# Attention over graph edges: the comparison that builds the incidence matrix reads its row of numbers from PSUM in place of SBUF

## The reference

```python
h = (x @ W).reshape(N, HEADS, HEAD_DIM)
e = leaky_relu(a_src[src] + a_dst[dst])          # one score for each edge and head
e = exp(e - segment_max(e, dst)[dst])
alpha = e / segment_sum(e, dst)[dst]
out = segment_sum(alpha[:, :, None] * h[src], dst)   # over the edges of each target node
```

## Time and profile before

| | us |
|---|---|
| median of 3 runs | 4344.1 (4341.25 to 4345.91) |
| the profiled execution, in all | 4370.65 |
| its span in the trace | 4368.8 |
| busy: PE 3282.1, DVE 2921.5, POOL 2098.1, ACT 1557.5 | |

### The profile page before, as it was taken

How to read it: one execution, slowest core, us unless ns; L and a number is a source line. 1 busy time by engine, 2 the same in 40 slices (tenths; PEclk the granted TensorE clock), 3 DMA queues, 4 the chain that set the end, 5 groups by cost and what they waited for, 6 DMA issues and landing times. The chain is left out here.

```text
span 4368.8 us, 73734 instructions
## 1 busy us (share of the span) xinstructions
PE 3282.1 (75%) x15898; PEld 2469.4 (57%) x15898; DVE 2921.5 (67%) x9594; ACT 1557.5 (36%) x4357; POOL 2098.1 (48%) x2122
## 2 busy tenths in 40 slices
PE   6477666677666789964566666666658999999999
PEld 4244444444444578853344444444437888888888
DVE  5598889888887866755556556556557765454554
ACT  3233333333332214432333333333333333333433
POOL 3777777777771024446777777777750000000000
PEclk9577777776776569987677777777779999999999
DMA  5344444444454137744444444444462000000000
GB/s 145 99 105 104 105 106 106 102 105 104 105 100 88 44 94 191 191 126 122 107 106 106 106 105 106 105 105 106 106 76 72 8 6 7 5 7 7 5 7 8
DMA packets 379249, 372.18 MB, mean 85 GB/s; under 512 B 246016, under 2 KB 305580, under 8 KB 378634
## 3 DMA queue, kind: packets, MB, share of 16 engines
q0 software_dynamic: 99072, 273.04, 25.3%
q1 hardware_dynamic: 277994, 94.55, 9.9%
q10 hardware_dynamic: 1818, 0.74, 0.1%
HBM read 326.48 MB, written 41.60 MB: 84 GB/s over the span
## 5 line engine op out<-in xcount | busy, mean ns | idle before, releaser
L781 POOL DMA_INDIRECT g_G<-rows,g_pack x1856 | 1830.0, 986 | 604.7 <-issue 476.9
L814 PE MATMUL bank<-g_G,g_MB 128*125 128x260 f32 x1856 | 679.6, 514 | 180.6 <-DVE acc L1020 179.4
L1020 DVE SCALAR_TENSOR_TENSOR acc<-acc,g_c,bank 125x65 f32 (+1 forms) x2320 | 618.0, 315 | 147.8 <-PE bank L814 72.2
L814 PE MATMUL bank<-g_G,g_M 128*125 128x257 f32 x1856 | 632.3, 488 | 20.7 <-DVE acc L1020 20.5
L814 PEld LDWEIGHTS bank<-g_G,g_MB 128*125 128x125 f32 x1856 | 433.0, 251 | 332.6 <-DVE acc L1020 212.6
L1318 ACT ACTIVATE e_h<-bank,bn_shift,bn_scale 128x250 f32<-128x250 f32 x800 | 401.3, 556 | 532.7 <-PE bank L1271 412.5
L885 ACT ACTIVATE g_mt_d<-bank,unode 125x256 bf16<-125x256 f32 x928 | 384.6, 464 | 507.9 <-PE bank L799 507.6
L814 PEld LDWEIGHTS bank<-g_G,g_M 128*125 128x125 f32 x1856 | 417.4, 241 | 147.3 <-DVE acc L1020 26.5
L1442 DVE SCALAR_TENSOR_TENSOR X<-bank,e_cw,X 125x256 f32 (+1 forms) x400 | 175.1, 479 | 408.4 <-PE bank L1280 406.2
L1280 PE MATMUL bank<-e_w,e_h 128*125 128x256 f32 x1400 | 334.2, 382 | 20.7 <-ACT e_h L1318 16.6
L919 ACT COPY g_LT<-bank 64x128 f32<-64x128 f32 (+1 forms) x116 | 29.8, 257 | 870.0 <-PE bank L829 862.3
(11 more groups left out here) (325 smaller groups left out, 4542.7 us busy)
## 6 DMA issues: line engine op xcount, KB each, us to landing
g_G<-rows,g_pack POOLq DMA_INDIRECT x1856
acc<-in_edge_attr SPq DMA_DIRECT2D x50, 476.0 KB
g_pack<-edge_pack SPq DMA_DIRECT2D x928, 2.0 KB
g_drow<-edge_dst SPq DMA_DIRECT2D x928, 1.0 KB
expert_out<-x_y SPq DMA_DIRECT2D x54, 256.0 KB
g_qe<-edge_q SPq DMA_DIRECT2D x464, 1.0 KB
rows<-acc SPq DMA_DIRECT2D x25, 227.5 KB
rows<-n_T SPq DMA_DIRECT2D x25, 224.9 KB
```

The source lines that it names most:

```text
L781: nc.gpsimd.indirect_dma_start(G[:, r, q, :], None, rows_d[l], bass.IndirectOffsetOnAxis(ap=pack[:, r, q, 0:1], axis=0)).then_inc(S(p + f" ...
L814: mm_ = nc.tensor.matmul(sum_bank(r, k, u)[0:TN, 0:HW], left, G[:, rk, q, :], start=(c == 0), stop=(c == C - 1))
L1020: ins = nc.vector.scalar_tensor_tensor(at, at, c1[:, rk, u, h:h + 1], sum_bank(r, k, u)[0:TN, h * W:(h + 1) * W], ALU.mult, ALU.add)
```

## The change

A copy of the row of numbers is put into PSUM, as fp32 at columns 128 to 252 of bank 7 (`iota_ps`), by one DVE instruction at the start of each attention, with a semaphore of its own. The four comparisons of each step then read `iota_ps` in place of `iota_b`. Bank 7 otherwise holds w_ps, in its first 64 or 16 columns. The second operand, dloc, and the output MB (fp32 for l = 0, bf16 for l = 1) stay in SBUF. No other instruction changes, and none is moved.

```diff
             w_ps = bank[7][:, 0:QH].rearrange("p (q h) -> p q h", h=H)
+            iota_ps = bank[7][:, P:P + TN]
...
                 @block.vector
                 def _(v):
+                    nc.vector.tensor_copy(iota_ps, iota_b[:, 0:TN]).then_inc(S(p + "iota"), 1)
                     nc.vector.memset(NEQ[:, :], 1.0)
...
                     v.wait_ge(S(p + "SA_set"), 2)
+                    v.wait_ge(S(p + "iota"), 1)
...
-                            nc.vector.tensor_tensor(MB[:, r, at, :], iota_b[:, 0:TN].unsqueeze(1).broadcast_to([P, CP, TN]),
+                            nc.vector.tensor_tensor(MB[:, r, at, :], iota_ps.unsqueeze(1).broadcast_to([P, CP, TN]),
                                                     dloc[:, r, at, 0:1].broadcast_to([P, CP, TN]), ALU.is_equal).then_inc(S(p + "MB"), 1)
```

## The result

| | before | after |
|---|---|---|
| median us (lowest to highest, 4 runs each) | 4343.85 (4341.25 to 4345.91) | **4313.82** (4308.81 to 4314.85) |
| ratio, 95% interval | | 0.9927 [0.9914, 0.9940] |
| the profiled execution (its span) | 4370.65 (4368.8) | 4308.81 (4307.1) |

The kernel is 30 us faster, 0.7%. The forecast was 63 us and its range began at 35, so the sign held and the size did not.

The account below looks back on a forecast made before the run. The prediction took POOL's gather chain, stretched by L1053's two SBUF operands, to bound both attentions. Gains of 40 us in attention 0 and 23 in attention 1 made 63 off the 4344.1 median: 4281 us, range 4270 to 4309.

Parts of the forecast that it names:

- Step 1: Start of each attention: copying iota into bank 7 is hidden by waits for packs; uncovered it would cost 0.5 us in all.
- Step 2: Comparison L1053 in both attentions: a PSUM source makes it 7 ns shorter, -0.03 us for the four of a step.
- Step 3: Gathers of both attentions: their stretch beside L1053, 68.6 us in all, goes away; mean about 950 ns, longest near 1000.
- Step 4: Attention 1: nothing else is near POOL's pace, so the whole 23.3 us of gather stretch is gained.
- Step 5: Attention 0: DVE's loop takes over at 20.22 us a step, just above POOL's 20.06, giving 40 us of at most 45.
- The 20.22: Attention 0: DVE's own loop in us a step after the change, 20.25 less the 0.03 of step 2.
- The 20.93: Attention 0 before the change: mean step of L1087 in us, over 53 steps of the profiled execution.
- The sum: Both attentions: 40 + 23 = 63 us off the profiled 4370.65 and equally off the median 4344.1, giving 4281 us.
- the first: Rival, attention 0: DVE's loop binds harder, L1053 40 ns longer, gaining 30 us there; 4291 us, chance 0.08.
- The second: Rival, attention 0: gives nothing because its 20.93 us a step are not POOL's doing; 4321 us, chance 0.06.
- POOL would begin to wait for slots there: Sign for step 5, attention 0: POOL's gathers start waiting for free slots, which they did not do before.
- 20.2 us and hardly vary: Sign for step 5, attention 0: L1087's steps come to 20.2 us with hardly any variation.

Follow-up runs that it names:

- before_fourth: The kernel before, unedited, executed once more with a trace: 4343.78 us, with 25.2 us of gather stretch in attention 0.
- act_lowers: Against the changed kernel, ScalarE takes the lowering of unit 0's sums in attention 0 from DVE's addition: 4314.38 us, ratio 0.9901 to the kernel before.
- after_again: The changed kernel, unedited, timed again beside the kernel before: 4312.26 us, ratio 0.9920.

## Why the prediction was right about the contention and wrong about its worth in attention 0

- **Step 1, the copy: hidden**, as said. It takes 0.29 us, and DVE still waits for the first pack of attention 0 behind it (3.7 us, 4.0 before).
- **Step 2, the duration of L1053: 671 ns, so -1 ns in place of -7**, 0.2 us in a stage. The rule of the Trainium skill that was weighed there (VectorE: DVE Perf Modes, "The TRN2 errata"), an estimate of 65 ns more, does not hold for this instruction: 671 ns with PSUM, 672 without.
- **Step 3, the stretch: gone.** The mean is 946 ns and the longest 1115, against "about 950" and "near 1000".
- **Step 4, attention 1: right**, 25 us for 23, in each kernel with the edit there.
- **Step 5, attention 0: this failed.** "Attention 0 gives 40 us" was 53 x (20.93 - 20.22), plus 2. Both numbers were off.
  - *The 20.22.* It came from two steps of 20.26 and 20.25, with the -0.03 of step 2, and took DVE's own loop to stay as it was. The changed kernel takes 20.48 over the same 53 steps, 20.35 in the median. That alone makes 53 x (20.93 - 20.48) + 2 = 26 of the 40, and the profiled executions differ there by 1209.7 - 1182.9 = 26.8 us.
  - *The 20.93.* It was one execution's: others had 20.50 and 20.54, so that 1 to 3 us are left over the 53 steps, and 3.5 and 5.7 between the gathers' spans (1186.4 and 1188.6 against 1182.9).
- **What made DVE's step longer** can be read from the traces. Set instruction by instruction beside the step before that starts at 870.65, the step after that starts at 857.43 is 0.11 us longer, and 0.10 of it lies at two places: behind L1096 (L1093 before) and at L1162 (L1159 before). L1096 is a short DVE instruction that ran free in nearly every step before, and now mostly ends with a gather. First its durations in attention 0 (ns min/median/max), before and after, then one of each in the timeline:

```profile
L1093 DVE TENSOR_SCALAR g_FB<-g_NEQ x57: 208/210/373, 140.9 to 1315.2; 64x128 f32<-64x128 f32 x57
L1096 DVE TENSOR_SCALAR g_FB<-g_NEQ x57: 208/320/431, 138.7 to 1287.1; 64x128 f32<-64x128 f32 x57
```

```profile
869.01 1.78 POOL L781 DMA_INDIRECT g_G<-rows,g_pack  x1 [0.30 <-issue]
870.98 0.21 DVE L1093 TENSOR_SCALAR g_FB<-g_NEQ 64x128 f32<-64x128 f32 x1
...
857.10 0.95 POOL L782 DMA_INDIRECT g_G<-rows,g_pack  x1 [0.30 <-PE bank L815]
857.76 0.32 DVE L1096 TENSOR_SCALAR g_FB<-g_NEQ 64x128 f32<-64x128 f32 x1
```

- In the changed kernel 35 of the 57 take over 0.25 us; all 35 start within a gather and end 0.04 to 0.05 us after it does. In the kernel before one of 57 does so. So the contention has a second direction, which the prediction did not look at: a gather can hold one of DVE's short instructions. No run tested this by itself. The rest of the way from 20.35 to 20.48 is mostly four steps of 21.3 to 21.7 us, in which DVE waits 1.6 to 1.8 us at L1110 for ScalarE in place of 0.70.
- **The sum: "I take the same 63 us off it" failed with it.** The 26.5 us between the profiled execution and the median were mostly stretch of attention 0, as far as the traces show: before_fourth, with 4343.78 us, is 26.9 us shorter, 23.3 of them in att 0. The prediction named this ("may lie in the gathers") and gave it 12 us at the high end of the range; attention 0 gave 35 less than the 40 there. With 25 us for attention 1 and 5 for attention 0 the sum is 30, as measured.
- The near agreement of 61.84 with 63 is partly chance: 26.8 + 25.1 of it lie in the gathers, and 10 in the stages around, where the two executions differ too.
- **Of the rivals**, the first had the right mechanism, DVE's loop binding harder, by a wrong cause (a longer L1053). The second, "attention 0 gives nothing", came nearest in time, 4321, and had 0.06. The view that spoke for it was there: 1040.3 us of DVE in the earlier trace rows, and two steps at 20.25 in the earlier trace rows, 0.2 us above POOL's 20.06, which show how little a longer DVE step would leave.
- **Of the signs**, "POOL would begin to wait for slots there" came true, with the 44 rests. "20.2 us and hardly vary" did not.

What stays open: why one execution of the kernel before has 25 us of stretch in attention 0 and another 46. Where POOL's gathers stand against DVE's comparisons should decide it, but what puts them there was not tested.

## What to carry to other kernels

Where two engines' loops are nearly as long (here 20.06 us of POOL and 20.48 of DVE), what is taken from the one is worth only the distance to the other. That distance is to be read as a mean over all steps, not from the smoothest ones, and the other loop can itself become longer when the first one moves against it. Before a gain is taken off a median, see whether the profiled execution is like those that make the median; a 26.5 us distance belonged to the very stage that was predicted. If the gain vanishes into the second loop, look for a wait in it that can be filled with other work: here moving one call gave 21 us more, which the same move could not give before.

## What was not expected of the hardware

A held gather does not wait in proportion: in attention 1 of the kernel before, it ends about 0.8 us after the instruction that holds it. In the earlier trace rows the L1053 that starts at 2320.80 ends at 2321.47 and the gather at 2321.03 + 1.26 = 2322.29, 0.82 us later. In the kernel with w in SBUF the scaling ends at 2282.61 + 0.67 = 2283.28 and the gather at 2282.94 + 1.16 = 2284.10, again 0.82 later. The 99 gathers over 0.97 us beside a comparison in attention 1 of the kernel before all end 0.81 or 0.82 us after it. A free gather takes 0.95 us in all, so a held one appears to do nearly all of its work once the other instruction is over.

It matters which of the two starts first. The 194 stretched gathers of the kernel before that overlap a comparison all started while one was running; of the 186 in which a comparison starts only after the gather has, none takes over 0.96 us. The other way round, DVE's short L1096 of the changed kernel took 0.32 us in place of 0.21 where it started late within a gather, and ended with it.

The kernel before took from 4341 to 4373 us in its runs here, and the changed one 4309 to 4315. Beside act_lowers, which has hardly any stretch (1.7 us in attention 0) and took 4312.78 to 4317.45 us in four executions, the kernel before took 4349.47 to 4372.52. But beside after_again, which took 4310.48 to 4314.67 us, its seven executions lay between 4345.16 and 4348.02. So the contention can go with a wide spread, and does not always; what decides it is open.
